# Scores and values issued as pieces of 32 columns on four column tiles of TensorE

## The reference, cut to what matters

```python
qkv = xw @ qkv_w.T + qkv_b                       # xw: windows x 49 tokens x 96
q, k, v = ...                                    # 12 heads of 8 channels
attn = jnp.einsum('bhqd,bhkd->bhqk', q, k) + bias[None]
attn = jax.nn.softmax(attn + mask, axis=-1)
out = jnp.einsum('bhqk,bhkd->bhqd', attn, v)
```

## Time and profile before

| what | value |
|---|---|
| median of three runs | 3227.89 us |
| the profiled execution's own time | 3227.62 us |
| its span, first to last instruction | 3225.8 us |
| mean granted TensorE clock | 0.986 |
| TensorE matmul busy | 3123.7 us, 97% |
| VectorE busy | 2870.6 us, 89% |
| ScalarE, GpSimd busy | 71%, 70% |
| DMA, share of 16 engines | some 34% |

### The profile page before, as it was taken

How to read it: one execution, slowest core, us unless ns; L and a number is a source line. 1 busy time by engine, 2 the same in 40 slices (tenths; PEclk the granted TensorE clock), 3 DMA queues, 4 the chain that set the end, 5 groups by cost and what they waited for, 6 DMA issues and landing times.

```text
span 3225.8 us, 195904 instructions
## 1 busy us (share of the span) xinstructions
PE 3123.7 (97%) x85120; PEld 2599.5 (81%) x85120; DVE 2870.6 (89%) x4882; ACT 2282.8 (71%) x4705; POOL 2267.8 (70%) x2522
## 2 busy tenths in 40 slices
PE   4999999999999999999999999999999999999997
PEld 3788888888888888888888888888888888888885
DVE  5899999999999999999999999999999999999983
ACT  2577777777777777777777777777777777777764
POOL 4577777777777777777777777777777777767763
PEclk8999999999999999999999999999999999999995
DMA  3333333333333333333333333333333333333320
GB/s 85 85 92 88 95 90 88 95 88 88 94 90 89 94 90 89 94 92 88 89 95 89 89 99 86 89 98 86 91 96 88 88 97 87 88 94 81 78 68 24
DMA packets 385888, 283.33 MB, mean 88 GB/s; under 512 B 261931, under 2 KB 384908, under 8 KB 385036
## 3 DMA queue, kind: packets, MB, share of 16 engines
q1 hardware_dynamic: 384652, 270.69, 34.2%
q10 hardware_dynamic: 384, 0.11, 0.0%
HBM read 39.35 MB, written 38.54 MB: 24 GB/s over the span
## 4 chain that ended last, share of the span: by engine, by line
PE 93%; ACT 3%; issue 2%; DVE 1%; ACTq 0%; SPq 0%; POOL 0%; DMA 0%; POOLq 0%; DVEq 0%
PE pP L472 23%; PE pO L488 16%; PE pS L460 12%; PE pM L556 6%; PE pM L573 5%; PE pM L511 5%; PE pM L442 5%; PE pM L562 5%; PE pM L394 3%; PE pM L501 3%; PE pM L400 3%; PE pM L401 3%; PE pM L402 3%; PE pM L582 2%; PE pM L529 1%
## 5 line engine op out<-in xcount | busy, mean ns | idle before, releaser
L1051 POOL TENSOR_TENSOR T<-T,MX 128x588 f32<-128x588 f32 x1024 | 1212.5, 1186 | 871.5 <-DVE MX L828 871.1
L663 ACT ACTIVATE P<-pP 128x588 f32<-128x588 f32 x1024 | 673.7, 658 | 413.0 <-PE pP L472 406.7
L821 DVE TENSOR_TENSOR T<-pS,table 128x588 f32<-128x588 f32 x1024 | 783.7, 765 | 85.4 <-PE pS L460 67.3
L472 PE MATMUL pP<-K,T 113*128 113x113 f32 x6144 | 820.0, 270 | 2.1 <-ACT P L663 1.0
L828 DVE TENSOR_REDUCE MX<-T 128x12 f32<-128x588 f32 x1024 | 778.3, 760 | 26.0
L472 PEld LDWEIGHTS pP<-K,T 113*128 113x128 f32 x6144 | 603.1, 141 | 95.4 <-issue 2.7
L488 PEld LDWEIGHTS pO<-V,P 128*17 128x17 f32 (+1 forms) x49152 | 505.6, 103 | 179.0 <-ACT P L663 69.2
L488 PE MATMUL pO<-V,P 128*32 128x18 f32 (+1 forms) x49152 | 610.5, 184 | 13.5 <-issue 12.5
L460 PE MATMUL pS<-KE,QS 128*64 128x196 bf16 (+1 forms) x8192 | 478.0, 234 | 19.9 <-DMA KE<-KS 14.3
L768 ACT ACTIVATE rd<-pM,tiny 112x384 f32<-112x384 f32 x224 | 130.2, 581 | 352.2 <-PE pM L562 352.1
L460 PEld LDWEIGHTS pS<-KE,QS 128*64 128x64 bf16 x8192 | 292.9, 109 | 53.2 <-DMA KE<-KS 14.5
(11 more groups left out here) (94 smaller groups left out, 5963.5 us busy)
## 6 DMA issues: line engine op xcount, KB each, us to landing
KE<-KS SPq DMA_DIRECT2D x512, 147.0 KB
KS<-knh SPq DMA_DIRECT2D x768, 49.0 KB
QS<-qnh SPq DMA_DIRECT2D x768, 49.0 KB
out<-tok_out SPq DMA_DIRECT2D x384, 84.0 KB
tok_in<-x SPq DMA_DIRECT2D x224, 84.0 KB
KS<-knl SPq DMA_DIRECT2D x384, 49.0 KB
QS<-qnl SPq DMA_DIRECT2D x384, 49.0 KB
tok_in<-x SPq DMA_DIRECT2D x224, 63.0 KB
```

The costliest lines, as they stand in the source:

```text
L472: mm = pe.transpose(pP[:, c, QN * at:QN * at + QN], T[j % 4][0:QN, 2 * h:2 * h + 2, :], pick)
L663: act.activation(P32[j % 3][:, :, :].rearrange("p (c a w) q -> p c a (w q)", c=2, w=2), src, ACT.Exp).then_inc(p_made, 1)
L821: dve.tensor_tensor(T[j % 4][:, :, 0:L].rearrange("p (b h) k -> p b h k", b=2), pS[:, :, 0:HALF].rearrange("p b (h k) -> p b h k", k=L), t ...
L1051: pool.tensor_tensor(t, t, MX[j % 4][:, :].unsqueeze(2).broadcast_to([128, HEADS, L]), ALU.subtract).then_inc(shifted, 1)
```

## The change

In `scores`, each matmul over 64 query columns becomes two over 32, the second with its output 32 partitions further down. In `values`, each matmul over 49 token columns becomes two over 32 and 17. `times_v` is as it was.

```diff
                             for h in range(2):
                                 wv = rhs[m % 2][:, :].rearrange("c (a h d) -> c a h d", h=2, d=D)
-                                mm = pe.matmul(bankA[64 * h:64 * h + L, col:col + C // 2], lhs, wv[:, :, h, :],
-                                               start=(part == 0), stop=(part == 2))
+                                for k0, k1 in ((0, 32), (32, L)):
+                                    mm = pe.matmul(bankA[64 * h + k0:64 * h + k1, col:col + C // 2], lhs[:, k0:k1],
+                                                   wv[:, :, h, :], start=(part == 0), stop=(part == 2))
...
-                        mm = pe.matmul(pS[64 * w:64 * w + 64, bank, col:col + (h1 - h0) * L],
-                                       Q[:, gq, at:at + 64], E[:, h0:h1, at:at + L], start=True, stop=True)
+                        for q0 in (0, 32):
+                            mm = pe.matmul(pS[64 * w + q0:64 * w + q0 + 32, bank, col:col + (h1 - h0) * L],
+                                           Q[:, gq, at + q0:at + q0 + 32], E[:, h0:h1, at:at + L],
+                                           start=True, stop=True)
```

## The result

The changed kernel takes 3627.28 us (median of four runs, 3619.03 to 3648.97), against 3226.72 before. The ratio is 1.1242, 95% interval 1.1212 to 1.1272. The forecast was 3187 us, with a range that ended at 3275: the sign was wrong, and the size by far.

The account below looks back on a forecast made before the run. TensorE, busy 97% of the span, was taken as the bound. From 3227.6 us, 50 saved in 768 steps without values and 10 lost in 256 with them gave 3187.6, stated as 3187; range 3120 to 3275, likeliest case 3150 to 3215.

Parts of the forecast that it names:

- The bound: Whole kernel: TensorE's order sets the time, busy 97% of the span; VectorE next, 918 of 1000 us.
- The seam: `times_v` to scores: the 0.10 us tile-form drain goes, at most 102 us; 0.065 us taken in 768 steps, 50 us.
- rival B: Scores: four bf16 streams don't fit; 3380 us at half rate, 3270 with three streams' worth; chance 0.17, half each.
- rival C: Values: each pair costs 13 ns whatever its tile, 161 us more, less 50: 3340 us; chance 0.06.
- Other costs: TensorE's issue of a quarter more pairs: 3 us more idle at `times_v`, anything beyond folded into the range.
- rival D: Seam stays 0.10 us for a reason other than tile form; values lose up to 0.20 a unit: 3270 us; chance 0.05.

Follow-up runs that it names:

- the woven order: Scores loops exchanged (head group first, window within), against the kernel with tiles of 64 in slots with values and 32 elsewhere: 3171.45 us, ratio 0.9820.

## Why the prediction was wrong

**The bound.** Right: TensorE set the time, and nobody else became the bound.

**The seam.** Right. A step without values saved 0.08 us where 0.065 was taken; and with the code held equal most of it reached the total (39 us of some 53).

**Four streams of bf16 (rival B).** They fit. In the changed kernel the scores span 0.248 us from first to last start (median), 0.214 before, the difference being the late start of the w = 1 tiles, which the woven order removes (0.210). The Trainium skill's 2.38 for three tiles (TensorE: Matmul & The Clock Gate, "Measured speedup vs the span model") is not borne out here: it would make three streams 0.06 us longer a step, and four cost 0.034 us more in the changed kernel's order and nothing when woven.

**The pair's pace (rival C).** 96 pairs of values take some 0.75 us without a stall (0.74 in the fastest unit, 91 in 0.72 us above; the median unit, stalls included, took 1.10), inside the forecast, not the 1.25 us of C. The Trainium skill's 25 ns from start to start, which the prediction puts under "What's actually happening", stands in the section behind it, "Wait — 56ns, not 53.3ns?". As a floor of one tile it agrees with the 26 ns of the values before; as one of the engine it does not, with under 8 ns a pair over four tiles.

**What failed** is the sentence under "Other costs": "TensorE's idle for issue at `times_v` is 12.5 us now, so a quarter more is 3 us". It scaled a threshold as if it were a rate. The words behind it, that late code would cost more and lies in the range, came without a price: no rival carried it, and the range ended at 3275. The runs put 56 us more idle at `times_v` (12.5 to 68.8) and 282 us more over all of TensorE's lines (19 to 301). Added up from the rows: seams -82 us (1024 x 0.08); values' own time 256 x 0.13 = +33; idle on "issue" +282; the lower clock, if work at half the clock takes twice as long, at most (268-95)/2 = +87; together +320 of the 408 us between the spans. An idle is only counted from the modelled end of the last matmul, some 0.2 us after its start (1804.62 against 1804.83); 307 more idles at that are 61 us, which leaves 27 unassigned. Even this sum mixes bounds and medians, so the parts are sizes, not a closed account.

One sum beside this is wrong and changes nothing: rival D's loss of up to 0.20 us a unit is 51 us, not 42, so its price would be 3279.

A look at what was there would have warned: the earlier trace rows show 85120 pairs, thus 170240 instructions or 10.9 MB of code in 3.2 ms, and the page's instruction queue its 677 packets; a step with values was to execute 160 pairs in 1.5 us, 20 KB, when a packet alone takes about 1 us.

## What to carry to other kernels

Splitting small matmuls into more tiles buys overlap with instructions, and code is a resource with its own supply: here some 2.4 us passed from a packet's start to its use where TensorE had to wait for it, and such a packet held 256 instructions. Before adding instructions to a dense burst, count the pairs that TensorE would execute in such a time, and look at idle "issue" and at the instruction queue. If a tile form is to be unified, choose per stretch the form with the fewer instructions where the code is dense, and the finer one where there is room, so that the total stays.

## What the runs showed of the hardware

- A change of column-tile form drained TensorE for 0.10 us; with it gone and all four tiles starting together, a step was 0.12 us shorter.
- Four column tiles streamed bf16 side by side, 588 columns each, with starts over 0.25 us, as two did over 0.21; started together, four took 0.21 as well.
- Stalls for code fell at the same place of every 256 instructions, ended a median 1.39 us after the packet, and also occurred in the kernel before: some 30 above 0.5 us, about 25 us in all.
- Stalls for code can cost again through the clock: 268 us at the 1.2 GHz level in the changed kernel, 95 before. They need not: scores alone in pieces had 83 us idle on "issue", none over 1.3 us long, and 91 us at that level.
